# Masked cross attention of a Perceiver-style kernel: its first 384 keys written out without rescaling, the rest in a loop of 512-key blocks

## The reference, cut to what matters

```python
xn = layernorm(x) * ln_gamma + ln_beta            # 256 x 256
q = xn @ Wq                                       # 16 heads x 64
k, v = split(context @ Wkv)                       # context: 4096 x 192
dots = where(mask, q @ k.T * 64 ** -0.5, -inf)    # mask: 256 x 4096, one byte each
x = x + softmax(dots) @ v @ Wo + bo
```

## Time and profile before

| | us |
|---|---|
| median of 3 runs | 459.45 |
| lowest, highest | 456.75, 459.59 |
| the profiled execution | 459.85 |
| its span, first to last instruction | 458.0 |
| PE busy in it | 429.9 (94%) |
| DVE, ACT, POOL busy | 276.7, 172.3, 6.3 |
| first cross attention, from the first keys to the output projection | 20.94 to 161.02 |

### The profile page before, as it was taken

The page is one execution under the profiler, slowest core; times in us unless marked ns, Lnnn a source line. Parts: engine busy times, 40 slices in busy tenths (PEclk is TensorE's granted clock), DMA queues, the critical chain, the costliest instruction groups (busy, mean ns, idle before and its releaser), DMA issues.

```text
span 458.0 us, 8353 instructions
## 1 busy us (share of the span) xinstructions
PE 429.9 (94%) x3124; PEld 308.5 (67%) x3124; DVE 276.7 (60%) x945; ACT 172.3 (38%) x443; POOL 6.3 (1%) x9
## 2 busy tenths in 40 slices
PE   2999999999999899977899999999899999899997
PEld 2645555555555488955658889888745669787774
DVE  7256676766767645687779989610325556465333
ACT  2346656646666502778322330000123233324110
POOL 5000000000000000000000000000000000000000
PEclk9999999999999899999999999999999999999999
DMA  8500000100005906200049800009493000000000
GB/s 297 156 2 1 1 0 2 34 2 1 1 1 186 370 4 243 124 1 3 1 137 375 286 1 5 1 3 308 102 358 111 1 0 3 0 1 0 1 1 23
DMA packets 21704, 36.09 MB, mean 79 GB/s; under 512 B 1694, under 2 KB 18464, under 8 KB 21024
## 3 DMA queue, kind: packets, MB, share of 16 engines
q1 hardware_dynamic: 21664, 35.55, 22.6%
HBM read 35.29 MB, written 0.26 MB: 78 GB/s over the span
## 4 chain that ended last, share of the span: by engine, by line
PE 49%; issue 42%; DVE 5%; ACT 2%; POOL 1%; POOLq 0%; DVEq 0%
PE bank L858 6%; PE bank L823 6%; PE bank L849 6%; PE bank L1056 6%; PE bank L945 5%; PE bank L920 3%; PE bank L925 2%; PE bank L1070 2%; PE bank L813 2%; PE bank L934 1%; PE bank L1074 1%; PE bank L709 1%; POOL region_d L1889 1%; DVE region_g L1522 1%; PE bank L724 1%
## 5 line engine op out<-in xcount | busy, mean ns | idle before, releaser
L1128 ACT ACTIVATE region_g<-bank,nm_new 128x512 f32<-128x512 f32 (+1 forms) x64 | 40.0, 630 | 35.9 <-DVE nm_new L1398 34.8
L1393 DVE CUSTOM_DVE_ANT_0 bank<-bank,bias_h 128x512 f32<-128x512 f32 (+1 forms) x64 | 38.7, 646 | 7.3 <-issue 7.3
L555 PEld LDWEIGHTS bank<-ident,region_g 128*128 128x128 f32 x230 | 24.5, 140 | 21.9 <-issue 12.8
L589 PE MATMUL bank<-region_a,qT 64*128 64x512 f32 (+1 forms) x128 | 32.5, 568 | 0.8 <-ACT region_g L1128 0.8
L555 PE MATMUL bank<-ident,region_g 128*128 128x128 f32 x230 | 32.5, 281 | 0.6 <-ACT region_d L1114 0.6
L348 ACT ACTIVATE root<-var 128x2 f32<-128x2 f32 x6 | 1.2, 204 | 80.4 <-DVE var L358 80.4
L572 PE MATMUL bank<-region_d,region_a 128*64 128x256 f32 x248 | 31.1, 390 | 0.0
L858 PE MATMUL bank<-region_u,region_g 128*128 128x256 f32 x128 | 28.7, 382 | 0.0
L1114 ACT COPY region_d<-bank 128x384 f32<-128x384 f32 (+1 forms) x50 | 24.8, 531 | 9.8 <-PE bank L555 9.8
L823 PE MATMUL bank<-xnT,region_d 128*128 128x256 f32 x128 | 28.0, 379 | 0.0
L823 PEld LDWEIGHTS bank<-xnT,region_d 128*128 128x128 f32 x128 | 24.2, 190 | 3.7 <-issue 0.5
(11 more groups left out here) (341 smaller groups left out, 796.1 us busy)
## 6 DMA issues: line engine op xcount, KB each, us to landing
region_d<-in_downT SPq DMA_DIRECT2D x2, 2048.0 KB, 9.7
region_u<-in_up SPq DMA_DIRECT2D x2, 2048.0 KB, 11.4
region_a<-in_ctx SPq DMA_DIRECT2D x1, 3072.0 KB, 13.5
region_d<-in_w_q SPq DMA_DIRECT2D x1, 2048.0 KB, 11.7
region_d<-in_ctxT SPq DMA_DIRECT2D x1, 2048.0 KB, 8.7
region_d<-in_ctxT SPq DMA_DIRECT2D x2, 1024.0 KB, 15.1
region_u<-in_wg SPq DMA_DIRECT2D x1, 1728.0 KB, 7.0
region_u<-in_wu SPq DMA_DIRECT2D x1, 1728.0 KB, 10.7
```

Of the source, the lines that this page charges most:

```text
L555: mm = nc.tensor.transpose(bank[4 + e][:, k * P:(k + 1) * P], prob[:, u % 2, e, k * P:(k + 1) * P], ident[:, :])
L589: mm = nc.tensor.matmul(bank[2 * s + e][:, 0:size], lhsT=qT[own, p, t * P:(t + 1) * P], rhs=keys[own, p, 0:size], start=True, stop=True)
L1128: nc.scalar.activation(prob[:, u % 2, e, 0:tiles * P], bank[2 * s + e][:, 0:tiles * P], ACT.Exp, scale=-1.0, bias=nm_new[:, p, t, e:e + 1] ...
L1393: ins = nc.vector.tensor_tensor_reduce(bank[2 * s + e][:, 0:size], bank[2 * s + e][:, 0:size], bias_h[:, t, 0:size], -1.0, 3e38, ALU.add, ...
```

## The change

- **First block.** The first 384 keys (`FIRST = 3` tiles) are written out ahead of the loop. It has no factors, no running maximum and no placeholders: `maxima` writes `nm_new` directly, the exponentials' sums go straight into `l_run` for pairs 0 to 5, and `first_values` copies PE's product to `o_acc` in one instruction. Its pairs 6 and 7 are finished in the loop as before, over four tiles, of which the fourth is zeros that POOL has set (`pads_set`).
- **Loop.** One block of 512 keys in each turn, `turn_factors` apart from `values`. For this mask it runs once.
- **Range.** The steps on DVE go from eleven to nine. The count of the groups (PE) moves from ahead of the query projection to behind its first output tile. The idle transposes go from 14 to 6.
- **DMAs.** The mask comes in two halves, ahead of the identity; Wq is issued ahead of columns. The first context load is 384 keys wide.
- **Small.** Shorter clears on DVE and POOL; PE starts its first keys without waiting for the last copy of the queries.

```diff
-TILES = (4, 3)
-OFFSET = (0, 4 * P)
-TURN = sum(TILES) * P
-PER = TURN // GRP
-NTURN = (GROUPS + PER - 1) // PER
+FIRST = 3
+PER = BLK // GRP
+BEGUN = FIRST * P // GRP
+NTURN = (GROUPS - BEGUN + PER - 1) // PER
...
+            for t in range(TT):
+                sp.dma_start(mask_w.bitcast(U32)[:, t, 0:S2 // 4], a["mask"][t * P:(t + 1) * P]).then_inc(mask_in[t], 16)
             sp.dma_start(ident[:, :], a["ident"]).then_inc(ident_in, 16)
-            sp.dma_start(mask_w.bitcast(U32)[:, :, 0:S2 // 4],
-                         a["mask"].rearrange("(t p) w -> p t w", p=P)).then_inc(mask_in, 16)
+            sp.dma_start(wq, a["Wq"].rearrange("(c p) n -> p c n", p=P)).then_inc(weights_in, 16)
             sp.dma_start(columns[:, :], a["columns"]).then_inc(columns_in, 16)
-            sp.dma_start(wq, a["Wq"].rearrange("(c p) n -> p c n", p=P)).then_inc(weights_in, 16)
...
-            for k in range(14):
+            for k in range(6):
                 nc.tensor.transpose(bank[3][:, k % 4 * P:(k % 4 + 1) * P], ident[:, :], ident[:, :])
...
+            pe.wait_ge(ctx_landed, 48)
+            keys_and_values(0, FIRST)
+            pe.wait_ge(q_ready, 4)
+            keys_and_values(1, FIRST)
+
+            def first_values(p):
+                if p >= 2:
+                    pe.wait_ge(o_added, p - 1)
+                values(p, FIRST, 0, 0)
+
+            for p in range(XP):
+                scores(p, 0, FIRST, 0, 0)
+                if p == XP - 1:
+                    first_values(p - 2)
+                if p >= 1:
+                    turn(p - 1, 1, FIRST, 0, 0)
+                if 2 <= p < XP - 1:
+                    first_values(p - 2)
+                scores(p, 1, FIRST, 0, 0)
+                turn(p, 0, FIRST, 0, 0)
+                if p + 2 < XP:
+                    keys_and_values(p + 2, FIRST)
+            pe.wait_ge(pads_set, 4)
             with pe.Fori(0, n_turns) as i:
...
+            copy_keys(0, FIRST, 0)
+            copy_keys(1, FIRST, 0)
+            act.wait_ge(pads_set, 4)
+            for p in range(XP):
+                sums = l_run if p < XP - 2 else l_blk
+                if p == XP - 1:
+                    exps(p, 0, FIRST, 0, 0, sums)
+                if p >= 1:
+                    for e in range(2):
+                        turned_half(p - 1, 1, e, FIRST, 0)
+                if p < XP - 1:
+                    exps(p, 0, FIRST, 0, 0, sums)
+                exps(p, 1, FIRST, 0, 0, sums)
...
+            set_bias(within(first * GRP, S2 - GRP), FIRST, 1)
+            copy_values(0, FIRST, 0)
+            copy_values(1, FIRST, 0)
+            for p in range(XP):
+                maxima(p, 0, FIRST, 0, nm_new).then_inc(nm_ready, 1)
+                if p >= 2:
+                    first_values(p - 2)
+                maxima(p, 1, FIRST, 0, nm_new).then_inc(nm_ready, 1)
+                turned_half(p, FIRST, 0)
+                if p + 2 < XP:
+                    copy_values(p + 2, FIRST, 0)
```

More of the change, by code:

```diff
@@ L450, in load_block @@
                                  ).then_inc(ctx_landed, 16)
-            load_block(within(first * GRP, S2 - GRP), 0)
+            load_block(within(first * GRP, S2 - GRP), FIRST)
             n_turns = sp.value_load(rng_i[0:1, 1:2], min_val=1, max_val=NTURN)
@@ L524, in _ @@
                     mm.then_inc(q_psum, 1)
+                if m == 0:
+                    pe.wait_ge(blocks_seen, 1)
+                    for t in range(TT):
+                        mm = nc.tensor.matmul(bank[2][0:1, 0:GROUPS], lhsT=ones[:, 0:1], rhs=seen[:, t, :],
+                                              start=t == 0, stop=t == TT - 1)
+                    mm.then_inc(blocks_counted, 1)
             def keys_and_values(p, tiles):
@@ L565, in values @@
                                         alpha[:, m, t].rearrange("p e d -> p (e d)"), ident[:, :])
+            def values(p, tiles, base8, base16):
+                m, into = p % XP, bank[6 + p % 2]
                 if p >= 0:
                     pe.wait_ge(v_ready, base8 + (KT_PER if p < KT_PER else XP))
-                pe.wait_ge(pT_even, base16 + (2 * p + 5))
-                pe.wait_ge(pT_odd, base16 + (2 * p + 5))
+                pe.wait_ge(pT_even, base16 + (2 * p + 2))
+                pe.wait_ge(pT_odd, base16 + (2 * p + 2))
                 for k in range(tiles):
@@ L618, in _ @@
+            end8, end16, end32 = n_turns * 8 + 8, n_turns * 16 + 16, n_turns * 32 + 32
+            turn_factors(-2, end8, end16)
+            values(-2, KT_PER, end8, end16)
+            turn(-1, 1, KT_PER, end16, end32)
             pe.wait_ge(l_ready, 1)
@@ new lines, in _ @@
+            dve.wait_ge(nm_ready, 2 * XP)
+            keep_maxima(1)
+            with dve.Fori(0, n_turns) as i:
+                base8 = dve.snap(i * 8 + 8)
+                base16 = dve.snap(i * 16 + 16)
+                base32 = dve.snap(i * 32 + 32)
+                set_bias(within(first * GRP + FIRST * P + i * BLK, S2 + FIRST * P - BLK), KT_PER, i + 2)
+                copy_values(0, KT_PER, base8)
+                copy_values(1, KT_PER, base8)
+                for p in range(XP):
+                    maxima(p, 0, KT_PER, base16, nm_blk).then_inc(nm_blk_ready, 1)
+                    running(p, 0, base16)
+                    add_sums(p - 2, base8, base16)
+                    add_values(p - 2, base8)
+                    maxima(p, 1, KT_PER, base16, nm_blk).then_inc(nm_blk_ready, 1)
+                    running(p, 1, base16)
+                    turned_half(p, KT_PER, base32)
+                    if p + 2 < XP:
+                        copy_values(p + 2, KT_PER, base8)
+                dve.wait_ge(diff_ready, base16)
+                keep_maxima(i + 2)
```

272 lines of the change are left out of this document (131 added, 141 removed).

## The result

| | before | after |
|---|---|---|
| median | 459.53 us (456.75 to 462.48, 20 executions) | 456.47 us (454.92 to 459.12, 20 executions) |
| ratio, 95% interval | | 0.9936 (0.9919 to 0.9954) |
| profiled execution, its span | 459.85, 458.0 us | 458.72, 456.9 us |
| mean granted clock of that execution | 0.995 | 0.993 |
| first keys start | 20.94 us | 21.32 us |

What follows compares the result with a forecast made beforehand. PE, busy 94% of the span, and what it waits for were taken as the bound. 1.1 + 4.9 + 1.3 - 3.4 = 3.9 us gained; against the 459.45 median the forecast was 455.5 us, range 452.8 to 458.8.

Steps and rivals of the forecast that it cites:

- Front: 1.1 us gained: Ahead of the first keys: they start at 19.8 instead of 20.94 us; bounds 1.6 gained to 0.3 lost.
- 16 matmuls in 7.43 us, 0.46 each: Query projection: it keeps before's rate, so with the count's 0.51 us it ends near 19.5 us.
- the projection stays at the lower level: Rival, front: with fewer idle transposes projection and count take about 15 us instead of 8; about 462 us; chance 0.06.
- PE work out and waits out, +6.2: First cross attention: 4.9 us gained from PE work taken out, 1.3 us from waits of the 384-key stage.
- waits in, -3.4: First pairs of the written block: without placeholders PE waits for exponentials; 3.4 us lost, between 2.1 and 4.4.
- the rival that the factors' slot returns nothing: Rival, pairs 2 to 7: DVE and ACT bind, so 0.31 us each become waits, 1.9 us; 457.4 us; chance 0.08.
- Pair 0: 2.7 forecast: Written block's first pair: PE waits 2.7 us before its turn, for the maximum, table load and exponentials.
- pair 1: 0.7 forecast: Written block's second pair: its turn ends 3.9 us after the scores began, against 3.2 of work; 0.7 us wait.
- the rival that it does not: Rival, pair 0: ACT runs the table load ahead of the maximum, the wait is 1.3 us less; 454.2 us; chance 0.22.
- costed at nothing: POOL's and DVE's shorter clears: no gain, since what follows waits for the identity and mask, which land later.
- The dip of the clock (0.20): Rival: PE's gap in the first pairs or front brings one stretch at 1.2 GHz, costing 1.7 us; 457.2 us; chance 0.20.

Runs made afterwards that it cites:

- b_front: The kernel before with only the change's front (transfer order, half masks, 6 idle transposes, count inside projection, nine range steps, later query wait); 460.83 us, ratio 1.0023.
- e_spare13: Experiment 2: the changed kernel with 13 idle transposes in place of 6 ahead of the query projection; 456.31 us, ratio to before 0.9916.
- e_columns_first: Experiment 4: the changed kernel with columns issued ahead of Wq again; 455.24 us, ratio to before 0.9915.
- e_slot: The changed kernel with 4 more idle transposes in each of pairs 2 to 6 of the written block; 462.02 us, ratio to before 1.0033.
- e_table_early: The changed kernel with one scratch exponential ahead of ACT's first-key copies, so the table loads there; 456.73 us, ratio to before 0.9943.
- experiment 10: The kernel before with GpSimd's four long clears moved behind the end of the normalisation; 461.79 us, ratio to before 1.0037.
- experiment 12: The kernel before with GpSimd's four long clears moved behind the end of the range's steps; 459.12 us, ratio to before 0.9990.
- e_block_only: Experiment 6: the changed kernel with before's transfer order, 14 idle transposes and count place; written block and shorter clears stay; 455.02 us, ratio to before 0.9906.
- b_clears_later: The same run as experiment 12: the kernel before with GpSimd's four long clears behind the range's steps; 459.12 us, ratio to before 0.9990.

## Why the prediction was right and where it was not

The time, 456.47, is 1.0 us above the forecast and inside its range. The closeness is in part luck: one term, the front's, came out with the wrong sign, and of the 3.1 us in the medians only 1.6 are work and waits at full clock, against 3.9 in the sum, in which nothing is won back from the clock. Its parts:

- **"Front: 1.1 us gained": this step failed.** The first keys came 0.4 us later than before in the profile, and the front alone cost 1.6 us at full clock (b_front). The landing of the columns and ACT's copies were nearly right (11.12 against 11.6 for the start of the projection). Wrong was the term "16 matmuls in 7.43 us, 0.46 each": that is the rate of a projection which 14 idle transposes had preceded without a gap. Behind six of them and a gap of 1.41 us it took 10.2 us with the count, not 7.9. The slow first matmuls also made the count and the range late (range set at 15.52, not 14.9). With e_spare13's count at nearly the same time (13.03 against 13.09) the context landed only for first keys at 20.24, so even a projection at full rate would have given about 0.7 us here, an estimate from that run, and not 1.1. The rival "the projection stays at the lower level" named this mechanism; it came in part, for 2.3 of its 7 us, and I had given it 6%. Experiments 2 and 4 remove it, by filling or by closing the gap.
- **PE work out and waits out, +6.2; waits in, -3.4: held.** First keys to output projection gained 3.3 us with one dip of the clock on either side, against 2.8 forecast. PE's busy time there fell by 4.8 us (4.9 forecast) and its idle time rose by 1.5 (2.1 forecast); the 512-key block has no wait left. The 512-key block took 71.28 (71 forecast), the written block 50.3 at clock 1.00 (50). By e_slot, PE's slots in pairs 2 to 6 count in full; the rival that the factors' slot returns nothing is out.
- **Pair 0: 2.7 forecast, 2.13 found; pair 1: 0.7 forecast, 0.35 found.** Two short waits that the sum lacks, 0.23 us for DVE's copy of v between pair 0's scores and 0.31 in pair 7, make it 3.0 of the 3.4 us. The order of the terms is right: maximum, table load, exponential. The table load waited, as the order of ACT's instructions said, and the rival that it does not is out; e_table_early takes exactly 1.28 us of the wait away. The turn began as soon as the first exponential allowed; its second head, which I had summed into the wait, shows only as 1.11 us for the six transposes at full clock instead of 0.88.
- **The clears "costed at nothing": right for the change, for a wrong reason.** Without long clears beside it DVE's chain is 1.6 us shorter (experiments 6, 10 and 12). In the change the late identity and then the late columns hide this. What it is worth in the kernel's time is open, since no run shortens the clears alone. It is the largest thing I did not see: the row of 1.69 us for 2 elements per partition, beside 0.16 to 0.17 for its neighbours, was in the trace of before.
- **The dip of the clock (0.20): it came in the profiled execution**, after pair 0, for 1.7 us by the clock and 1.3 us in the block's time; in 14 of 32 executions of after the mean clock was 0.999 or more, so it did not come there at all. Before has dips too (0.999 in 6 of 79), so the kernel as a whole lost less to the clock than before, not more.

At full clock the front alone costs 1.6 us (b_front, 458.3). What it lacks, the block and the shorter clears, brings that down to after's 455.0: 3.3 us, where 2.8 was forecast, and as much as the profiles show between first keys and output projection. With the front of before, block and clears give 4.9 (e_block_only). That is 1.6 more, because there the clears are no longer hidden and the missing wait for the queries' copy counts in as well (in b_front it is part of the front); how the two share it no run shows.

The Trainium skill (ScalarE: Activation LUTs, What ACT_TABLE_LOAD costs) adds a drain of 1.38 us to each switch of tables. No run here shows it: the exponential starts at 30.01, right behind 28.71 + 1.28, and the wait shrank by 1.28 when the load was moved.

## What to carry to other kernels

The rate of a stretch of matmuls belongs to what stands ahead of it: when idle work is cut or a transfer is moved so that PE gets a gap at the start of a kernel (1.04 to 1.87 us in the slow cases here, 0.61 and 0.16 in the fast ones), price the work behind the gap at the lower rate, and look at the time of one matmul, since the granted clock's column may not show it. Look for instructions that take many times what their neighbours of the same size take, and at what another engine does until they end; moving the long clear only moves the wait, shortening it (as here) removes it. A table load belongs ahead of a wait, where the engine is idle anyway; and before an improvement of a microsecond is believed, set the medians beside what each execution lost to its clock.

## What the runs showed that was not expected

- **VectorE waits for GpSimd's clears, whole.** A TENSOR_SCALAR on 128x2 took 1.69 us, one on 128x128 2.05 (0.23 without), a COPY of 128x2 2.83 (0.17 without); the last two ended 0.07 and 0.02 us behind the end of GpSimd's clear of region_d, the first beside the end of the following one (5.54 + 0.95 = 6.49, var's end 6.51). TENSOR_REDUCE was not held (2.29 us beside clears, 2.28 without). The waiting goes the other way too: the clear of region_a took 1.51 us instead of 0.95 in b_clears_later, until DVE's bias ended at 19.13. The Trainium skill (SBUF — State Buffer, Who interferes with whom) has it that the two engines share a pair of ports as an exclusive lock, that copies and TENSOR_SCALAR can contend for it and reductions on trn2 never do; by that rule the trace agrees, in all five of these rows. A RECIPROCAL and a TENSOR_TENSOR of 128x2 were not held either: 0.17 and 0.16 us at 13.81 and 14.01 in b_clears_later, beside the clear of region_g (13.71 to 14.66).
- **The granted clock's column does not show the slow start.** It reads 1.00 from 6 to 20 us in before, after and all twelve experiments, while records of one shape took 0.51 us apiece at 11 us (after) and 0.225 at 12 us or later (e_columns_first). That the clock is the cause is therefore argued from the rate, not read. The end of the slow stretch is not at a fixed place either: in two executions of the same code the last 28 records of the projection took 7.88 and 6.76 us.
- **A clock kept up in one place did not lower the loss over the whole.** With pair 0's gap filled the clock held there and the average loss was 2.2 us; with 20 transposes more in the block it was 3.8, again with the clock at 1.00 in the profiled block. Whether these differ by more than chance, and why, is open.
